# Counting the dst ids of a sorted edge list: one-hot digits made by 21 comparisons with constants, and fifteen ids to a matrix product

## What is computed

```python
x = layernorm(x + L0(x, src, dst))      # mean of x[src] @ W_in.T over each dst, mean of x[dst] @ W_out.T over each src, then a GRU cell
x = layernorm(x + L1(x, stack([src, dst]), edge_attr_64))
# L1: relu(concat(h[row], h[col], bond) @ W1 + b1) @ W2 + b2, times sigmoid(bond @ Wa + ba), summed by row, plus h
```

## Time and profile before

| | us |
|---|---|
| median of 3 runs (lowest to highest) | 13822.69 (13819.65 to 13827.88) |
| span of the profiled execution | 13804.0 |
| last instruction of DVE in the first stage ends | 124.06 |
| first transfer of the next stage issued | 125.06 |

### The profile page before, as it was taken

How to read it: one execution, slowest core, us unless ns; L and a number is a source line. 1 busy time by engine, 2 the same in 40 slices (tenths; PEclk the granted TensorE clock), 3 DMA queues, 4 the chain that set the end, 5 groups by cost and what they waited for, 6 DMA issues and landing times. The chain is left out here.

```text
span 13804.0 us, 248896 instructions
## 1 busy us (share of the span) xinstructions
PE 8659.3 (63%) x53687; PEld 7672.6 (56%) x53688; DVE 8365.0 (61%) x29393; ACT 2711.9 (20%) x7251; POOL 9686.8 (70%) x10125
## 2 busy tenths in 40 slices
PE   3777775333333333333577777797878888888886
PEld 2555554333333333333577777556777777777775
DVE  6555555666666666666677777654444455444444
ACT  0000000111111111111000000153444444444443
POOL 3777775777777777777777777306777777777774
PEclk9555555555555565656788888898999999999998
DMA  5822222666666666666677767513333334333336
GB/s 179 307 54 54 54 54 69 199 200 197 200 197 198 198 198 198 198 199 197 175 186 187 187 182 189 101 45 81 79 80 79 80 88 95 80 80 79 80 80 82
DMA packets 2665835, 1886.18 MB, mean 137 GB/s; under 512 B 1375879, under 2 KB 2460455, under 8 KB 2664868
## 3 DMA queue, kind: packets, MB, share of 16 engines
q1 hardware_dynamic: 1505354, 806.75, 22.0%
q0 software_dynamic: 377360, 782.89, 19.5%
q10 hardware_dynamic: 782662, 292.60, 8.7%
HBM read 1509.53 MB, written 483.44 MB: 144 GB/s over the span
## 5 line engine op out<-in xcount | busy, mean ns | idle before, releaser
L1806 POOL DMA_INDIRECT p<-q_rows,small x3432 | 3241.7, 945 | 1645.7 <-issue 1001.8
L1011 PE MATMUL bank<-p,ring 128*128 x6656 | 1551.7, 427 | 2740.1 <-DVE ring L958 2736.8
L1011 PEld LDWEIGHTS bank<-p,ring 128*128 128x128 f32 x6656 | 1439.3, 328 | 2852.5 <-issue 2852.4
L1070 POOL DMA_INDIRECT edges_a<-ring,small x1664 | 1633.9, 982 | 593.1 <-issue 455.7
L1070 POOL DMA_INDIRECT edges_b<-ring,small x1664 | 1631.9, 981 | 507.2 <-issue 450.5
L805 POOL DMA_INDIRECT ring<-in_x,ring x1664 | 1569.9, 943 | 533.4 <-issue 530.1
L1844 PE MATMUL bank<-ring 128*128 128x256 f32 x3432 | 1199.8, 435 | 761.0 <-DVE p L1756 758.9
L836 PE MATMUL bank<-ring 128*128 128x129 f32 x3328 | 1239.5, 491 | 613.9 <-DMA ring<-in_x,ring 542.1
L1212 POOL DMA_INDIRECT ring<-in_x,small x1352 | 1275.8, 944 | 467.6 <-issue 409.1
L1232 PE MATMUL bank<-p,ring 128*128 128x129 f32 x8360 | 1217.2, 316 | 539.0 <-DVE ring L1160 538.9
L1232 PEld LDWEIGHTS bank<-p,ring 128*128 128x128 f32 x8360 | 1179.7, 230 | 577.3 <-issue 577.2
(11 more groups left out here) (285 smaller groups left out, 13425.4 us busy)
## 6 DMA issues: line engine op xcount, KB each, us to landing
p<-rows_by_slot SPq DMA_DIRECT2D x418, 928.0 KB
p<-edges_b SPq DMA_DIRECT2D x530, 262.0 KB
p<-edges_a SPq DMA_DIRECT2D x520, 262.0 KB
bonds_by_dst<-in_bond ACTq DMA_DIRECT2D x5, 20625.0 KB, 159.9
ring<-edges_a ACTq DMA_DIRECT2D x1792, 33.0 KB
p<-q_rows,small POOLq DMA_INDIRECT x3432
ring<-edges_b ACTq DMA_DIRECT2D x1664, 33.0 KB
ring<-bonds_by_dst ACTq DMA_DIRECT2D x1672, 32.0 KB
```

Source lines behind the costliest of these rows:

```text
L1011: last = nc.tensor.matmul(found[q][:, j, :], hot_t[g % GRPS][:, QUAD * h + j, :], x, start=True, stop=True, skip_group_check=True)
L1070: pool.indirect_dma_start(out=c.edges[s], out_offset=bass.IndirectOffsetOnAxis(ap=pos[:, k:k + 1], axis=0), in_=rec[:, k, :], in_offset=No ...
L1806: pool.indirect_dma_start(out=gath[g][:, k, :], out_offset=None, in_=c.q_dram, in_offset=bass.IndirectOffsetOnAxis(ap=gidx[g][:, k:k + 1], ...
```

## The change

The digits of all ids are taken at once by two DVE instructions into int32 (`whole`), and ACT casts them to bf16 (`digits`). The one-hots are laid out with the digit outside and the ids inside, so that each of the 21 digit values (13 and 8) is one DVE comparison of 660 bf16 digits with a constant. There are 5 steps of 660 ids instead of 30 of 110. A product takes 15 ids that lie `APART` = 44 apart: v is now the stationary operand (120 columns), u the moving one (195 columns), both read in steps of 44 elements of bf16, which is 88 bytes. There are 220 products instead of 660, and the loops are written out. The comparison of neighbours is made ahead of the counting and written as bf16; PE sums it over the partitions in ten products of 330 columns, and DVE adds the 330 sums. The weight and blank-row transfers of ACT come behind its two casts.

```diff
-HC, CG = 110, 5
+HC, CG = 660, 15
+APART = HC // CG
@@ scalar
             act.dma_start(c.consts[:, :], ins["consts"]).then_inc(s_const, 16)
+            for k in range(2):
+                act.wait_ge(s_digit, k + 1)
+                nc.scalar.copy(digits[k], whole[k]).then_inc(s_cast, 1)
...
@@ vector
+            dve.wait_ge(s_ids[1], 32)
+            nc.vector.tensor_scalar(whole[0], raw[:, 1, 0:TT], 10, None, ALU.logical_shift_right).then_inc(s_digit, 1)
+            nc.vector.tensor_scalar(whole[1], raw[:, 1, 0:TT], 7, 7, ALU.logical_shift_right,
+                                    ALU.bitwise_and).then_inc(s_digit, 1)
...
-            dve.wait_ge(s_ids[1], 32)
-            with dve.Fori(0, HSTEPS // 2) as i:
...
-                    for dig, hot, width in ((digits[0], us[n], HU), (digits[1], vs[n], HV)):
-                        nc.vector.tensor_tensor(
-                            hot, dig.unsqueeze(2).to_broadcast([TP, HC, width]),
-                            c.iota[0:TP, 0:width].unsqueeze(1).to_broadcast([TP, HC, width]),
-                            ALU.is_equal).then_inc(s_dig, 1)
+            dve.wait_ge(s_edge, 16)
+            nc.vector.tensor_tensor(after, raw[:, 1, 0:TT], raw[:, 1, 1:TT + 1], ALU.is_gt).then_inc(s_viol, 1)
+            dve.wait_ge(s_cast, 2)
+            for i in range(HSTEPS):
+                n = i % 2
+                if i >= 2:
+                    dve.wait_ge(s_cnt, i - 1)
+                for dig, hot, width in ((digits[0], us[n], HU), (digits[1], vs[n], HV)):
+                    for d in range(width):
+                        nc.vector.tensor_scalar(hot[:, d, :], dig[:, i * HC:(i + 1) * HC], float(d), None,
+                                                ALU.is_equal).then_inc(s_dig, 1)
+            dve.wait_ge(s_cnt, HSTEPS)
...
-            step.link(nc.vector.tensor_tensor(after[:, 0:TT], raw[:, 1, 0:TT], raw[:, 1, 1:TT + 1], ALU.is_gt))
-            nc.vector.reduce_sum(viol, after[:, 0:TT], AXX).then_inc(s_viol, 1)
             dve.wait_ge(s_flag, 1)
+            step.link(nc.vector.reduce_sum(viol, c.bank[2][0:1, 0:HC // 2], AXX))
@@ tensor
+            for i in range(HSTEPS):
+                n = i % 2
+                pe.wait_ge(s_dig, (HU + HV) * (i + 1))
+                v = vs[n].rearrange("p d t -> p (d t)")
+                for t in range(APART):
+                    last = nc.tensor.matmul(cross, v[:, t:HC * HV:APART], us[n][:, :, t:HC:APART],
+                                            start=(i == 0 and t == 0), stop=(i == HSTEPS - 1 and t == APART - 1))
+                last.then_inc(s_cnt, 1)
+            pe.wait_ge(s_viol, 1)
+            for t in range(0, TT, HC // 2):
+                last = nc.tensor.matmul(c.bank[2][0:1, 0:HC // 2], c.ones[0:TP, 0:1], after[:, t:t + HC // 2],
+                                        start=(t == 0), stop=(t == TT - HC // 2))
+            last.then_inc(s_flag, 1)
             pe.wait_ge(s_cross, 1)
             for t in range(CG):
-                last = nc.tensor.matmul(counts, c.ident[0:CG * HU, t * HU:(t + 1) * HU],
-                                        cross_s[:, t * HV:(t + 1) * HV], start=(t == 0), stop=(t == CG - 1))
+                last = nc.tensor.matmul(counts, cross_s[:, t:CG * HU:CG], c.ident[0:CG * HV, t:CG * HV:CG],
+                                        start=(t == 0), stop=(t == CG - 1))
```

More of the change, by code:

```diff
@@ L226, in load_constants_and_count @@
     pairs = c.pairs()
-    after = scratch[:, 7000:7000 + TT // 2].bitcast(BF16)
-    digits = [scratch[:, 9000 + 200 * n:9000 + 200 * n + HC].bitcast(I32) for n in range(2)]
-    us = [scratch[:, 9600 + 750 * n:9600 + 750 * n + HC * HU // 2].bitcast(BF16).rearrange("p (t d) -> p t d", d=HU)
-          for n in range(2)]
-    vs = [scratch[:, 11200 + 500 * n:11200 + 500 * n + HC * HV // 2].bitcast(BF16).rearrange("p (t d) -> p t d", d=HV)
-          for n in range(2)]
+    after = c.blk_s[0:TP, 0:TT]
+    digits = [scratch[:, 6610 + k * (TT // 2):6610 + (k + 1) * (TT // 2)].bitcast(BF16) for k in range(2)]
+    top = 6610 + TT
+    whole = [scratch[:, top + k * TT:top + (k + 1) * TT].bitcast(I32) for k in range(2)]
+    us = [scratch[:, top + n * (HC * HU // 2):top + (n + 1) * (HC * HU // 2)].bitcast(BF16)
+          .rearrange("p (d t) -> p d t", d=HU) for n in range(2)]
+    vs = [at.bitcast(BF16).rearrange("p (d t) -> p d t", d=HV)
+          for at in (c.part(7200, HC * HV // 2)[0:TP, :], c.tab[0:TP, 0:HC * HV // 2])]
+    assert top + HC * HU <= (NB + 1) * XW and 7200 + HC * HV // 2 <= RINGW and HC * HV // 2 <= S_COLS
     spare = 2 * TT
@@ L311, in _ @@
             nc.vector.tensor_copy(c.iota_b[:, :], c.iota).then_inc(s_z, 1)
-            dve.wait_ge(s_ids[1], 32)
-            with dve.Fori(0, HSTEPS // 2) as i:
-                step.loop(i, 4)
-                for n in range(2):
-                    ids = raw[:, 1, bass.ds((2 * i + n) * HC, HC)]
-                    dve.wait_ge(s_cnt, 2 * i + n)
-                    step.mark(nc.vector.tensor_scalar(digits[0], ids, 10, None, ALU.logical_shift_right))
-                    step.link(nc.vector.tensor_scalar(digits[1], ids, 7, 7, ALU.logical_shift_right, ALU.bitwise_and))
-                    for dig, hot, width in ((digits[0], us[n], HU), (digits[1], vs[n], HV)):
-                        nc.vector.tensor_tensor(
-                            hot, dig.unsqueeze(2).to_broadcast([TP, HC, width]),
-                            c.iota[0:TP, 0:width].unsqueeze(1).to_broadcast([TP, HC, width]),
-                            ALU.is_equal).then_inc(s_dig, 1)
-                    dve.wait_ge(s_dig, 4 * i + 2 * n + 2)
@@ L326, in _ @@
-            step.end(HSTEPS // 2)
+            dve.wait_ge(s_edge, 16)
[9 more added lines that the diff above has]
+                                                ALU.is_equal).then_inc(s_dig, 1)
@@ L340, in _ @@
         def _(pe):
-            pe.sem_inc(s_cnt, 1)
             pe.wait_ge(s_z, 8)
-            nc.tensor.matmul(cross, zero16[:, 0:1].to_broadcast([TP, CG * HU]),
-                             zero16[:, 0:1].to_broadcast([TP, CG * HV]), start=True, stop=False)
-            with pe.Fori(0, HSTEPS // 2) as i:
-                for n in range(2):
-                    pe.wait_ge(s_dig, 4 * i + 2 * n + 2)
-                    for t in range(0, HC, CG):
-                        last = nc.tensor.matmul(cross, us[n][:, t:t + CG, :].rearrange("p t d -> p (t d)"),
-                                                vs[n][:, t:t + CG, :].rearrange("p t d -> p (t d)"),
-                                                start=False, stop=False)
-                    last.then_inc(s_cnt, 1)
```

22 lines of the change are left out of this document (9 added, 13 removed).

## The result

The changed kernel takes **13941.49 us** in the median (13936.21 to 13969.66, four runs), the kernel before 13825.28 beside it (13819.65 to 13835.06, four runs): 1.009 times as long, 95% interval 1.0076 to 1.0104. It is slower by 116 us, where 55 less were predicted. The profiled execution is the longest of its four (13969.66), some 28 us above their median, while the profiled span of the kernel before is a short one.

The account below looks back on a forecast made before the run. DVE's one-hot comparisons were taken to set the first stage; with PE bounding the changed one, its end moves from 124.1 to 69.4 us, and 13822.7 - 54.7 = 13768 us, range 13750 to 13790.

Parts of the forecast that it names:

- Everything behind the barrier is unchanged and starts that much sooner.: All stages after the first: same lengths as before, only shifted earlier by the first stage's saving of 54.7 us.
- at nothing, hidden while PE lags: First stage: instruction fetch of the written-out loops was put at no cost.
- the sum is wrong as a whole if the next stages do not simply shift: Closing sign, stages behind the first: if they do more than start earlier, the whole forecast fails; no size.
- the 4% for new waits: First stage: some other new wait there, up to 40 us; chance 4%.
- the price of a product, 0.172: First stage, PE: each of 220 products takes 0.172 us, 7.6 a step, so PE becomes the bound.
- Slower than before: Rival, first stage's product operand reads: new lines make products exceed 0.42 us each, 2.2 ns a column; chance 2%.
- The prediction's 0.50 at 300 to 350 us: Clock column in a later stage, PE busy 34.35 of 50 us: cited for the clock reaching 2.4 GHz.
- PE goes fast: Rival, first stage: 2.4 GHz and free 88-byte steps, 3.7 us a step, DVE bounds, saving 66 to 70; 32%, partly fast included.
- L311 at 12.0 and 1.85 each: First stage, DVE's two digit instructions on 3300 ids: the first starts at 12.0 us, each takes 1.85.
- The comparisons near 21 and 0.245 apart: First stage, DVE's 105 one-hot comparisons: start at 20.9 us, 0.245 each, 25.7 in all.
- The tail, 5.0: First stage, from the last product to DVE's end: sums, copies, flag and hops together 5.0 us.
- The change doesn't move the end: Rival, first stage: SP's other transfers or the load of src end last; rejected because they land by 58 us.

Follow-up runs that it names:

- e4: The changed kernel with added groups of 30 products and six comparisons, each with another operand layout; ran once, 13918.03 us, only its rows are read.
- e6: The changed kernel with one-hots laid out as 44 groups of [digit][15 ids], so both product operands are dense; 13867.85 us, 1.0032 times the kernel before.
- e11: e6 with 9 one-element DVE memsets added in a branch never taken; 13744.85 us, 0.9943 times the kernel before.

## Why the prediction was wrong

**What failed first, and cost most: "Everything behind the barrier is unchanged and starts that much sooner."** Of the 173 us between forecast and result, some 112 arise there and 61 in the stage. The prediction did count the written-out loops, and put their fetch "at nothing, hidden while PE lags"; that holds within the stage, where no stall shows. It didn't ask where those 84 to 87 instructions push the loops behind them. The rows that could have raised the question were in the trace of before: 51 issue waits at L965, one for each turn but the first, 103.6 us in all, and 26 at L1171. They say that DVE pays for its loops already, and an edit that changes the length of DVE's program can move that payment. The text ended with "the sum is wrong as a whole if the next stages do not simply shift", which is what happened, and gave it no chance of its own beyond the 4% for new waits "in the stage".

**What failed second: the price of a product, 0.172.** The step was "I take the slow price for all [...] either because the clock stays low or because the steps cost what a doubled clock would give." Measured is 0.447, 2.3 ns a column. The term was mis-sized by 220 x 0.275 = 61 us, and the stage came out at +6.3 instead of -54.7. The rival "Slower than before" had the right mechanism and the right break-even price, 0.42 each or 2.2 ns a column, and asked that the load be exposed too; it wasn't, since with the load alone in steps a product takes 0.228 (e4). I gave it 2%, "for it only that no row has such steps". With no row, a factor of 2.6 above the price taken wasn't excluded by anything. The Trainium skill's rule from "SBUF — State Buffer", in its section on the DMA port swizzle, that each access to another 16-byte line pays a penalty, spoke for the rival, and it was used for a factor of two only, though it has no figure. The trace agrees that each new line costs; it doesn't agree that two hits on a line are enough. By the runs a product costs twice the dense price of 0.086 at steps of 8 bytes (two reads on a line, clock at 1.00), four times at 16 and 32 bytes, and five times at 88 (clock at 0.50).

**The clock.** The prediction's 0.50 at 300 to 350 us rests on this row of the kernel before, which stands in the windows view:

```profile
300.00:350.00 50.00, 34.35 (x160) 26.72 (x160) 28.52 (x64) 0.00 (x0) 37.81 (x41) 0.50 0.99 347
```

Its reading that the clock may stay at 1.2 GHz in this stage was right. The ten products of 330 columns that follow the counting take 2.91 us in the changed kernel, 0.88 ns a column, and 1.58 in e6; yet the profile's column reads 1.00 from 26 to 129 us, where it can't be taken at its word. But the clock isn't what set the price (e4). In e6, dense, the first step's products take 5.87, as the first 24 of them run at 0.16 each, and 4.01 from the third step on (195 columns in 0.091 us, more than 1.2 a ns, so the level is 2.4 GHz): with dense operands the "PE goes fast" rival, 32%, is what happens. It put DVE as the bound, 3.7 for a step's products and 53.8 for the end; e6 shows 4.01 and 54.9. Its other half, that steps of 88 bytes cost nothing, is refuted.

**What was right.**
- DVE's comparisons bound the stage before, and PE after; DVE waits from the third step on.
- L311 at 12.0 and 1.85 each: 11.56, and 2.16 and 1.86 for the two. The start was near by luck: the profile puts the wait down to the ids of dst, which the prediction had in at 9, and not to POOL's clearing, which ended at 11.99. The comparisons near 21 and 0.245 apart: 21.48 and 0.241. This was the least certain of DVE's terms, bounded by 0.245 and 0.41, and the nearer row was the right guide.
- The tail, 5.0: from the last product at about 125.3 to 129.8, 4.5.
- The neighbour comparison starts at 17.97, 0.7 late, behind a wait of 0.82 for the shifted column. ACT's casts (2.94 each) end before the comparisons can start, and the pairs' store is hidden. Its issue is at 34.4, not 41.6 to 47.2: the stalled issue of the earlier trace rows didn't come back when the transfers moved to 15.5. That error cost nothing.
- "The change doesn't move the end" was excluded for the right reason.

The two faults add up, and either alone would have spoiled the forecast. With the count dense, as the fast rival had it, the kernel is still 43 us slower than before (e6) at the place where the edit happened to leave DVE's code, and some 78 us faster (e11) nine instructions further on.

## What to carry to other kernels

Before pricing an edit that writes out or shortens a loop, look for issue waits that come once per turn in later loops: by the account above they mark loops that are fetched anew in each turn, and a shift of some instructions changed what they cost, here by up to 123 us of 13,800. Compare two versions at several places (pad by instructions in a branch never taken), or the place is measured instead of the edit. And lay one-hots out so that each product reads dense rows; writing runs of 15 bf16 costs DVE no more than dense rows (0.26 us for 660 elements), and the dense product is five times as fast as one read 88 bytes apart (0.086 and 0.447).

## What the runs showed of the hardware that was not expected

- The instruction queue's packets count the turns: 270 in `sort_records`, some 5 per turn, in the kernel before, and 14 or 15 at place 93 to 96, as if the loop's code were not fetched again (183 packets in all against 437 to 464).
- A DVE write of bf16 in runs of 15 costs 0.26 us for 660 elements, as dense; in 55 runs of 12 it costs 0.42, in steps of 16 bytes 1.53 (e4).
- The granted clock can fall while PE is busy without a gap. In e4 it is 1.00 to 134 and 0.50 from 135 on, in the middle of the products whose stationary operand alone is read 88 bytes apart; it is 1.00 again from 156 on, behind the 4-byte steps, and 0.50 from 166 on, within the 16-byte steps. In the changed kernel some 99 us of gapless products read 88 bytes apart left it at 1.2 GHz, as the ten products behind them show. PE's busy share alone doesn't tell the clock.
- Steps of 88 bytes cost 0.228 us a product on the stationary operand alone (120 columns, 1.9 ns each) and 0.446 on the moving one alone (195 columns, 2.3 ns each); on both they cost 0.447 in the changed kernel, so the cheaper one is hidden behind the other.
